# Staging the operands of dense attention through device memory, with a new order of work around it

## What is computed

```
q1, k1, q2, k2, v = (einsum('btc,hcd->bhtd', x, w) for w in (wq1, wk1, wq2, wk2, wv))
w1 = softmax(einsum('bhtd,bhsd->bhts', q1, k1) * hs ** -0.5, axis=-1)
w2 = softmax(einsum('bhtd,bhsd->bhts', q2, k2) * hs ** -0.5, axis=-1)
out = einsum('bhts,bhsd->bhtd', w1 - lamb * w2, v)
```

## Time and profile before

| | us |
|---|---|
| median of 3 runs | 5161.87 |
| lowest, highest | 5161.16, 5163.03 |
| the profiled execution | 5163.37 |
| its span in the trace | 5161.6 |
| PE busy in the span | 4068.8 (79%) |
| VectorE busy | 3241.6 (63%) |
| ScalarE busy | 2677.9 (52%) |
| GpSimd busy | 1247.6 (24%) |

### The profile page before, as it was taken

How to read it: one execution, slowest core, us unless ns; L and a number is a source line. 1 busy time by engine, 2 the same in 40 slices (tenths; PEclk the granted TensorE clock), 3 DMA queues, 4 the chain that set the end, 5 groups by cost and what they waited for, 6 DMA issues and landing times. The chain is left out here.

```text
span 5161.6 us, 126690 instructions
## 1 busy us (share of the span) xinstructions
PE 4068.8 (79%) x45549; PEld 2390.4 (46%) x45678; DVE 3241.6 (63%) x5957; ACT 2677.9 (52%) x5510; POOL 1247.6 (24%) x2886
## 2 busy tenths in 40 slices
PE   2004767876768889596997578999999999999997
PEld 1003333432332222243443336777777777777775
DVE  7996434554437677444555327777777777777775
ACT  2024723554546767361224445666666666666664
POOL 0010200111201111110000144444444444444443
PEclk7556977997879989796998679999999999999998
DMA  2000020000010000001442001000000000000000
GB/s 57 0 0 1 2 69 23 2 1 1 1 33 1 1 2 1 11 2 49 140 135 61 5 9 42 6 10 25 6 28 6 6 28 6 10 24 6 28 6 11
DMA packets 60834, 110.23 MB, mean 21 GB/s; under 512 B 11399, under 2 KB 43251, under 8 KB 59164
## 3 DMA queue, kind: packets, MB, share of 16 engines
q1 hardware_dynamic: 59558, 101.70, 6.7%
q0 software_dynamic: 784, 1.80, 0.2%
HBM read 96.06 MB, written 1.74 MB: 19 GB/s over the span
## 5 line engine op out<-in xcount | busy, mean ns | idle before, releaser
L676 DVE TENSOR_REDUCE minus_max<-banks 128x1 f32<-128x512 f32 (+4 forms) x1152 | 606.1, 570 | 321.6 <-PE banks L571 315.2
L641 ACT ACTIVATE probs<-banks 128x512 f32<-128x512 f32 (+4 forms) x1152 | 581.0, 556 | 339.1 <-PE banks L609 336.8
L2961 POOL TENSOR_TENSOR loc_cos_part<-loc_cos_part,loc_sin_part 128x512 f32<-128x512 f32 x388 | 495.0, 1276 | 658.3 <-DVE loc_sin_part L3390 657.8
L3034 PE MATMUL banks<-loc_w_qkv,loc_shifted 128*128 128x256 f32 x1552 | 389.2, 394 | 15.1 <-DMA loc_adder_of<-loc_head_ones 15.1
L609 PE MATMUL banks<-q_stack,k_stack 64*128 64x512 bf16 (+3 forms) x1152 | 254.5, 381 | 98.9 <-DMA q_stack<-max_rows 71.4
L3423 DVE TENSOR_TENSOR loc_headsT<-banks,loc_sum_inv 128x512 f32<-128x512 f32 x192 | 132.7, 691 | 279.0 <-ACT loc_sum_inv L3295 279.0
L3034 PEld LDWEIGHTS banks<-loc_w_qkv,loc_shifted 128*128 128x128 f32 x1552 | 282.2, 192 | 53.8 <-DMA loc_w_qkv<-in_L_ffn_Wqkv_dram 15.5
L622 PE MATMUL banks<-probs,pair_rows 128*32 128x512 f32 (+3 forms) x2304 | 296.1, 590 | 0.0
L3415 DVE TENSOR_REDUCE loc_minus_max<-banks 128x4 f32<-128x384 f32 x386 | 197.1, 552 | 151.1 <-PE banks L3101 150.4
L700 POOL CAST max_parts<-minus_max 128x8 bf16<-128x8 f32 x192 | 36.7, 191 | 1038.0 <-DVE minus_max L676 1038.0
L1987 PE MATMUL banks<-identity,srt_b 128*128 128x128 f32 x64 | 11.2, 320 | 344.5 <-DVE srt_b L2267 344.5
(11 more groups left out here) (524 smaller groups left out, 9405.0 us busy)
## 6 DMA issues: line engine op xcount, KB each, us to landing
expert_share<-limited_rows SPq DMA_DIRECT2D x136, 256.0 KB, 3.9
expert_w<-in_L_ffn_pairs_dram SPq DMA_DIRECT2D x84, 192.0 KB, 2.3
loc_w_qkv<-in_L_ffn_Wqkv_dram SPq DMA_DIRECT2D x7, 1536.0 KB, 7.8
expert_share<-grouped_rows SPq DMA_DIRECT2D x32, 256.0 KB, 3.9
q_stack<-max_rows SPq DMA_DIRECT2D x384, 3.0 KB
loc_v_edge<-loc_v SPq DMA_DIRECT2D x192, 32.0 KB, 1.8
fixed_w<-in_L_ffn_experts_dram SPq DMA_DIRECT2D x8, 514.5 KB, 3.6
loc_pack<-in_L_ffn_pack_dram SPq DMA_DIRECT2D x6, 537.5 KB, 4.1
```

The lines of the kernel that those rows point to most:

```text
L641: nc.scalar.activation(probs[(a % 2) * C + k][e][0:kn, q0:S], t_bank[e][0:kn, q0:S], ACT.Exp, scale=scale).then_inc(s["exp_done"], 1)
L676: nc.vector.tensor_reduce(minus_max[:, u, e, qs[0]:qs[0] + len(qs)], view, AX.X, ALU.max, negate=True).then_inc(s["max_done"], 1)
L2961: nc.gpsimd.tensor_tensor(cos_part[:, tiles, :], cos_part[:, tiles, :], sin_part[:, tiles, :], ALU.add).then_inc(s["summed"], 1)
L3034: ins = nc.tensor.matmul(g.bank[3 * j][:, (t % 2) * QK:(t % 2 + 1) * QK], xs[:, t * P:(t + 1) * P], w_qkv[:, ds(at, QK)], start=True, stop ...
```

## The change

- A class `Stacks` holds two buffers, each with the stacks of a whole batch (8 pairs), and an image of the pieces in device memory. `store` writes the pieces of a batch there, six DMAs; `load` fetches them into place, four DMAs of 48 rows x pairs x keys or queries; `load_bias` adds the bias rows, two DMAs. The rows that hold ones are filled by GpSimd in `project`. The selection matmuls, their evacuations and their constants go.
- `project` gets work on SP: it stores batch 0 once its pieces are split, and loads pairs 0 and 1, then pairs 2 to 7.
- `attend` is written out for all 32 pairs without a loop. SP also stores later batches and loads the next one, between the sends (six stores and loads in a causal or context call, twelve and two in the calls of the differential stage).
- Direct products run three pairs ahead (four in context stages). Maxima are turned and sent two pairs ahead, with two `max_rows`.
- Three banks for turned and three for direct products. In a unit the turned product of head i stands beside the direct product of head 1 - i.
- Value products are cut into halves of 256 queries, at fixed places. `pair_rows` is doubled, and so is `probs` for pairs of even number, in context stages all of it (eight cleared buffers instead of four).
- In context and causal stages, `keep_awake` puts a product of 256 columns behind each direct product ahead of the loop, whose result is not used.
- `clear(nc, stacks.s)` is one more block after each of the five stages.

```
+    def store(self, sp, batch, sem, rows=slice(0, P)):
...
+        for slots, pieces in ((slice(0, 3), slice(0, 3)), (slice(3, 5), slice(0, 2)), (slice(5, 6), slice(0, 1))):
+            sp.dma_start(q_dram[rows, slots, q], q_parts[rows, pieces, q]).then_inc(sem, 16)
+        for slots, piece in ((slice(0, 3), 0), (slice(3, 5), 1), (slice(5, 6), 2)):
+            sp.dma_start(k_dram[rows, slots, k], k_parts[rows, piece:piece + 1, k].to_broadcast(
+                [count, slots.stop - slots.start, self.nk])).then_inc(sem, 16)
+    def load(self, sp, batch, pairs, sem):
...
+        for e in range(2):
+            rows = slice(64 * e, 64 * e + MAX_ROW)
+            for stacks, dram, n in ((self.q, self.drams[i][0], S), (self.k, self.drams[i][1], self.nk)):
+                src = dram.rearrange("(a e d) s t -> e (d s) a t", e=2, d=DH)[e][:, pairs, b * n:(b + 1) * n]
+                sp.dma_start(stacks[batch % 2][rows, pairs, 0:n], src).then_inc(sem, 16)
...
+def project(nc, g, projections, values, stacks):
...
+                sp.wait_ge(s["third_ready"], 2)
+                stacks.store(sp, 0, stacks.s["first_stored"], slice(0, 2 * DH * 2))
+                stacks.store(sp, 0, stacks.s["stored0"], slice(2 * DH * 2, P))
+                sp.wait_ge(stacks.s["stacks_filled"], 2 if stacks.biased else 1)
+                sp.wait_ge(stacks.s["first_stored"], 96)
+                stacks.load(sp, 0, slice(0, 2), stacks.s["first_loaded"])
+                if stacks.key_bias is not None:
+                    stacks.load_bias(sp, 0, stacks.key_bias)
+                sp.wait_ge(stacks.s["stored0"], 96)
+                stacks.load(sp, 0, slice(2, PAIRS), stacks.s["loaded0"])
...
+                for u in range(2):
+                    nc.gpsimd.memset(stacks.k[u][:, :, :], 1.0).then_inc(stacks.s["stacks_filled"], 1)
+                    if stacks.biased:
+                        nc.gpsimd.memset(stacks.q[u][:, :, :], 1.0).then_inc(stacks.s["stacks_filled"], 1)
...
+    AHEAD = 4 if context else 3
+    SENT_AHEAD = 2
+    VALUES_OWN = {7: (0, 0)} if context else {13: (0, 0), 14: (0, 1)}
+    VALUES_NEXT = ({1: (0, 1), 2: (1, 0), 3: (1, 1)} if context else
+                   {1: (1, 0), 3: (1, 1), 5: (2, 0), 6: (2, 1), 7: (3, 0), 9: (3, 1)})
+    ROWS_AT = (1, 5) if context else (4, 12)
...
+                    if which == 0:
+                        if n == 0:
+                            load_next(sp, 1)
+                        if n % 4 == 1 and 1 <= n // 4 and n // 4 + 1 < batches:
+                            stacks.store(sp, n // 4 + 1, stacks.s[f"stored{n // 4 + 1}"])
+                    b, a = divmod(n, PAIRS)
+                    if b and a == 2 and which * B + b + 1 < batches:
+                        load_next(sp, which * B + b + 1)
...
+                def slot(n):
+                    for k in range(C):
+                        for i in range(2):
+                            if not plain:
+                                turned_masks(n, k, i)
+                                if ahead < N:
+                                    direct_masks(ahead, k, i)
+                            turned(n, k, i)
+                            if ahead < N:
+                                direct(ahead, k, i)
```

More of the change, by code:

```diff
@@ L430, in project, with attend @@
         clear(nc, s)
-def attend(nc, g, q_parts, k_parts, rows, out, context, causal=False, key_bias=None, mask=None):
+def attend(nc, g, stacks, which, rows, out, context, causal=False, key_bias=None, mask=None):
     nk = CTX if context else S
@@ L489, in after @@
         def after(engine, name, count):
[L491 removed]
+            if count > 0:
                 engine.wait_ge(s[name], count)
[L494 to L503 removed]
@@ L710, in _ @@
             def _(sp):
[L711 to L719 removed]
+                batches = B * len(stacks.parts)
@@ new lines, in _ @@
+                if key_bias is not None and stacks.key_bias is None:
+                    stacks.load_bias(sp, 0, key_bias)
+                if which == 0:
+                    stacks.store(sp, 1, stacks.s["stored1"])
+                for n in range(N):
+                    sp.wait_ge(s["rows_done"], n + 1)
+                    for e in range(2):
+                        row = 64 * e + max_row
+                        sp.dma_start(stacks.q[batch_of(n) % 2][row:row + 3, n % PAIRS, :],
+                                     max_rows[n % 2][3 * e:3 * e + 3, :]).then_inc(s[f"sent{n % 2}"], 16)
+                    if which == 0:
+                        if n == 0:
[5 more added lines that the diff above has]
+                        load_next(sp, which * B + b + 1)
@@ new lines, in turned @@
+                def turned(n, k, e):
+                    q_stack, k_stack = stacks_of(n)
+                    k0 = ktiles[k][0]
+                    q0 = k0 if causal else 0
+                    rows_e = slice(64 * e, 64 * e + max_row + 3)
+                    if k == 0 and e == 0:
+                        pe.wait_ge(s[f"sent{n % 2}"], 32 * (n // 2 + 1))
+                    if plain:
+                        after(pe, "exp_done", unit(n, k, e) - 2)
+                    nc.tensor.matmul(t_bank(n, k, e)[:, q0:S], k_stack[rows_e, k0:k0 + P], q_stack[rows_e, q0:S],
+                                     start=plain, stop=True, skip_group_check=True).then_inc(s["turned_ready"], 1)
@@ new lines, in _ @@
+                for n in range(AHEAD):
+                    for k in range(C):
+                        for i in range(2):
+                            if not plain:
+                                direct_masks(n, k, i)
+                            direct(n, k, i)
+                            if context or causal:
+                                keep_awake()
+                    if 0 < n <= SENT_AHEAD:
+                        turn_rows(n - 1)
+                for n in range(N):
+                    slot(n)
@@ L951, in remembered_attention_1 @@
             clear(nc, s)
-        attend(nc, g, q_parts, k_parts, rows, out, context=True, key_bias=flat_bias(key_bias))
+        attend(nc, g, stacks, 0, rows, out, context=True, key_bias=key_bias)
+        clear(nc, stacks.s)
         finish(nc, g, "heads", out, w["o"])
@@ L1129, in context_attention_2 @@
         clear(nc, fetched)
-        attend(nc, g, q_parts, k_parts, rows, out, context=True, mask=mask)
+        attend(nc, g, stacks, 0, rows, out, context=True, mask=mask)
+        clear(nc, stacks.s)
         finish(nc, g, "heads", out, w["o"], b_o)
```

639 lines of the change are left out of this document (285 added, 354 removed).

## The result

The changed kernel takes 5115.11 us (median of 4 runs, 5103.21 to 5118.54) against 5162.02 before (4 runs): a ratio of 0.9905, 95% interval 0.9888 to 0.9922. It is faster by 47 us where 288 were forecast, and lies outside the stated range of 4795 to 4985. The profiled execution has a span of 5113.6 us, 48.0 less than before.

A forecast was written before the change was run, and what follows sets the result against it. Attention blocks were taken as bound by coupling between engines and by sends. Savings of 154, 50, 100 and 15 us (unrounded 318), plus 22 and 8 us added, gave -288 and 4874 us; 8-in-10 range 4795 to 4985.

The forecast's parts named there:

- rates read at the full clock: All blocks: back-to-back times from the trace, such as 0.60 us a row maximum and 0.23 us for two products.
- sums by engine: Attention blocks: each engine's work per pair added up, the busiest taken as bound; plain VectorE 5.1, PE 4.9, ScalarE 4.8 us.
- Causal: Causal block: PE bound at 6.0 us a pair, 6.25 taken; 214.6 against 264.9 us, -50.
- Biased contexts: Two biased context blocks: 3.1 us a pair taken, 12 us for late sends; 128.4 against 177.5 and 178.8, -100 together.
- Masked context: Masked context block: 5.0 us a pair on PE, 5.1 taken; 178.1 against 192.7 us, -15.
- Plain blocks: Two plain 512-key blocks: VectorE bound, 5.35 us a pair; 190.7 against 267.8 and 267.7 us, -154 together.
- rival B: Sends behind staged transfers: 8 ns a run instead of 5.6 makes sends late, +97 us, 4971; chance 0.07.
- Rival A: PE: unequal products don't overlap, 5015 us, chance 0.10; weaker form, engines losing time to each other, 4925 to 4985, 0.12.
- Rival C: Attention blocks: transfers so dear they bound them, slower than before; 5320 us at 14 ns a run; chance 0.03.
- D: Attention blocks: floors of 5.15, 6.0 and 2.85 us a pair, no stall; about 67 less, 4807 us; chance 0.05.
- The rest of the program: Outside attention blocks: projections +22 us for staged transfers, semaphore clears +8, first stage with fewer constant loads 0.
- The price of a run: Staged transfers: 5.6 ns a run, from an issue held some 11.5 us by 2048 runs at the kernel's start.

The follow-up runs named there:

- e6: Changed kernel with PE by step in causal and context blocks, and copy of maxima and head transposes moved in contexts: 4884.42 us, ratio 0.9472.
- e7: e6 with each batch's load in two halves behind two sends, its store likewise: 4820.54 us, ratio 0.9348.
- e8: e7 with causal, first context and masked block by unit again, second context's copy and transposes at old places: 4992.78 us.
- e2: Changed kernel with 16 unused products ahead of the loop in the first context and causal block, order by unit: 5087.61 us.
- e4: Changed kernel without stores and loads after batch 0 in five blocks; causal by unit with 16 fillers, contexts' moves, second context and masked by step: 4866.46 us.
- e5: Changed kernel with different edits by block (order by step, moves, fillers); second context moves only the copy of the maxima: 4917.01 us.
- e1: Changed kernel with PE by step in causal and masked block, and copy of maxima and head transposes moved in biased contexts: 4907.56 us.
- e3: Changed kernel without the causal block's masks and without the context prologues' filler products: 4975.14 us.
- e9: e7 with causal and masked block's masks together but products alternating by unit, and no fillers in the first context: 4820.37 us.

## Why the prediction was wrong, point by point

**The steps that failed: rates read at the full clock, used for whole blocks, and sums by engine where two engines wait for each other.** Every duration of the sum came from rows at or near the full clock (1.00 in the stretches of the earlier trace rows, 0.89 to 0.95 over the blocks of the earlier trace rows). The prediction had the clock column of the earlier trace rows in front of it and gave it no term. With PE 90% to 96% loaded in the forecast (2.8 of 3.1, 6.0 of 6.25 us), this term could take most, and no rival had it. Two edits that change only the order bring 5115.11 to 4884.42, which is as much as 231 of the 241 us missed. The causal block gives 123 of them, by its clock. The three context blocks give 44, 25 and 36, where lock step, order and clock were not fully parted.

That e6 ends within 11 us of the forecast of 4874 is luck as a sum: from the first maximum its plain blocks are still some 40 us above the forecast, its masked block is some 20 below, and the rest of the program is below too.

**Causal.** Of the 127.8 us missed here 12 lie ahead of the first exponential, which came 24.6 us after the block's start where 12.5 were forecast, with PE at 0.50 and full. The rest is the rate of the pairs. The cost of scattered masks was counted as time (0.12 us a unit for changes of shape, 1 us a pair). At full clock that was fair: 5.7 us a pair by unit without transfers, 5.2 by step in e7. What was not counted is that this order, once at the lower clock, does not leave it: 9.3 us a pair. Shown by e8 against e7, with e2 and e4 for the other half: it holds the full clock until a gap of 2.24 us. Which property of the mix the chip responds to is open. The runs show that in the causal block this order keeps the clock down and masks together or none let it rise; in the masked block the same order does not keep it down (e8).

**Biased contexts.** "I take 3.1" rested on engine sums and missed a lock step between two engines over one bank: turn at place 5, copy behind the exponential of place 6, transposes at place 6. A pair took 4.9 and 4.2 us. It should have been found in the order of the change: for each PE wait, the place at which ScalarE fills it. In the second context the transposes' move is worth 15 us (151.3 in e5, 136.5 in e1). With both, and with the load halved, a pair takes 3.0 us.

**Masked context.** 193.7 us against 178.1. The pair was right in size (5.0 us, 5.1 forecast), but by luck: the lock step is in it, and without it and by step it takes 4.0. The start was mis-sized: the first exponential comes 19.4 us after the block's start and not 12.5, at a clock of 0.50.

**Plain blocks.** 213.9 and 206.3 us from the first maximum, about 189 forecast. A pair takes 5.3 to 5.4 us without late sends (5.35 forecast) and 5.6 with them. The first exponential comes 15.6 us after the block's start, as forecast (15.1), but what follows was mis-sized: until 1625 us PE runs at 0.50, with a wait of 5.6 us in it, for the first send behind a load.

```profile
1605.00:1625.00 20.00, 14.40 (x81) 3.82 (x79) 11.81 (x20) 10.59 (x21) 1.93 (x10) 0.51 0.38 51
1625.00:1645.00 20.00, 19.39 (x194) 6.46 (x196) 18.25 (x33) 17.70 (x35) 3.45 (x18) 1.00 0.24 81
```

Transfers were costed as hidden and cost 14.0 and 9.8 us (e4).

**Transfers (rival B).** The mechanism was right, the price was too low and not where the prediction had it: 24 us were forecast in the blocks, and halving the transfers alone gave back 67 in the span (e6 to e7). Each transfer was set against its own send. In the order of SP a store (behind every fourth send) and a load (behind the third send of a batch) follow one another, so one send stands behind both, as at 938.47 in e2, and the slack of 5.2 us in the longer blocks is not enough. In e6's first context PE waited 14.6 us in five waits, up to 5.3 each, against 12 forecast for the block; in the plain blocks of the changed kernel it waited 11.2 and 4.6 us, against 0. The page "DMA: Bandwidth & Descriptors" of the Trainium skill, section "Queues, rings and completion order", says rings are consumed in order; e4 and e7 agree with it (14.6 to 3.5 us of waits in this block by halving what stands in front, none without transfers).

**Rival A** (no overlap) fell: the two products start 0.01 us apart. **Rival C** did not come near. **D**, floors everywhere at 4807, is near where e7 ended, at 4820.54, but not by D's terms: e7's causal pair takes 5.2 us and not 6.0, its plain pair 5.3 and not 5.15. D's "about 67 less" also comes out of its own terms as some 60.

**The rest of the program.** -24 against the forecast: 30 us were added for projections and semaphores, and the stretches outside the blocks grew by 6.5. The first `project` starts its VectorE work at 467.1 us instead of 474.0. The prediction gave the removed constant loads (two of 768 KB on GpSimd's queue) 0, and they are the likely source of these 6.9 us, though no run takes them out alone. The other 17 us were not traced. The price of a run was too high in the same place: the issue held for 11.45 us in the earlier trace rows is held for 4.31 now, which by the prediction's own working is 2.1 ns a run instead of 5.6. So its row had probably other traffic in it.

```profile
4.67 0.90 SPq L1979 DMA_DIRECT2D x_tokens<-in_x_dram  x1
5.62 4.31 SPq L1980 DMA_DIRECT2D ctx_transposed<-in_ctxT_dram  x1
```

## What to carry to other kernels

Where a forecast has PE nearly full (90% and more here), give its clock a term of its own: ask for each reordered stretch whether it starts at the lower clock and what would raise it, and price the stretch at both levels. Keep short products of one shape together, and measure both orders: in the causal block this gave 134 us by the clock, in the masked one by unit and by step differed by 23.5 us at nearly the same clock. When an order is written out by hand, walk each wait between two engines by places before summing their work, and put nothing long on the queue of a small transfer that PE waits for, or cut it into pieces that fit the slack.

## What the runs showed of the hardware

PE's granted clock can stay at 0.50 with PE busy all the time: 336.2 of 337.5 us in e8. A busy share near 100% is thus no sign that the clock will rise. The Trainium skill, "TensorE: Matmul & The Clock Gate", tells in the section "What's actually happening" that activity releases the throttle, and in "HAM oscillation — how this bites in real kernels" warns of idle gaps. The traces agree that a gap matters (clock 1.00 ahead of it and 0.50 behind in e2), but at 2.24 us it is shorter than those that the page warns of. They don't agree that activity is enough: in the causal block the clock came back 14 to 23 us behind the first exponential with the masks together or left out (e1, e3, e9), and not in over 300 us with them apart. In the masked block it came back in either order. The same instructions in two orders differ by 134 us in a block of 203.
